# Bringing the 32-by-32 blocks of a turned node pair with eight 128-partition transfers instead of four 32-partition ones, in a graph layer on one Trainium2 core

## What is computed

```python
msg  = x[src]
agg  = segment_sum(msg, dst, num_segments=n)
deg  = segment_sum(ones, dst, num_segments=n)
mean = agg / maximum(deg, 1)[:, None]
h    = mean @ W_l + b + x @ W_r
x    = layernorm(x + h * sigmoid(h))
```

## Time and profile before

| | |
|---|---|
| time, median of 3 runs | 1550.5 us (1549.07 to 1550.78) |
| the profiled execution's own time | 1550.07 us |
| its span, first to last instruction | 1548.2 us |
| granted TensorE clock, mean of the span | 0.989 of full speed |
| PE busy in the span | 1501.8 us (97%) |
| DVE, ACT, POOL busy | 1319.6, 1184.4, 1030.7 us |
| bytes moved by DMA | 397.68 MB, mean 257 GB/s |

### The profile page before, as it was taken

The page is one execution under the profiler, slowest core; times in us unless marked ns, Lnnn a source line. Parts: engine busy times, 40 slices in busy tenths (PEclk is TensorE's granted clock), DMA queues, the critical chain, the costliest instruction groups (busy, mean ns, idle before and its releaser), DMA issues.

```text
span 1548.2 us, 23957 instructions
## 1 busy us (share of the span) xinstructions
PE 1501.8 (97%) x7198; PEld 1244.3 (80%) x7198; DVE 1319.6 (85%) x2088; ACT 1184.4 (77%) x1609; POOL 1030.7 (67%) x1097
## 2 busy tenths in 40 slices
PE   7799999999999899999999999999999999999996
PEld 6687778888887787888888888888888888888884
DVE  7699999999998777888888888888888888888886
ACT  4354433333334698999999999999999999999996
POOL 6466556656662766667767777677677776776673
PEclk9899999999999999999999999999999999999998
DMA  5656589989997689999999999999999999999995
GB/s 193 173 178 192 166 247 266 266 259 272 267 267 232 176 258 265 277 283 276 276 271 268 280 298 270 281 287 273 268 281 281 289 280 279 280 277 275 290 270 184
DMA packets 298965, 397.68 MB, mean 257 GB/s; under 512 B 42652, under 2 KB 144822, under 8 KB 298837
## 3 DMA queue, kind: packets, MB, share of 16 engines
q1 hardware_dynamic: 250855, 321.43, 69.6%
q0 software_dynamic: 46944, 74.22, 18.0%
q10 hardware_dynamic: 1038, 0.50, 0.1%
HBM read 335.97 MB, written 139.67 MB: 307 GB/s over the span
## 4 chain that ended last, share of the span: by engine, by line
PE 80%; ACT 5%; DMA 5%; issue 4%; DVE 4%; POOL 1%; SPq 1%; POOLq 0%; ACTq 0%; DVEq 0%
PE pH L529 72%; PE pT L633 4%; PE pT L602 3%; DMA cor<-correction_rows,node_idx 2%; ACT O L804 2%; ACT cor L750 1%; PE pT L540 1%; ACT pH L816 1%; DMA X<-in_x 1%; POOL cor L441 1%; DMA light_x<-in_x 1%; DVE Z L904 1%; ACT Z L828 0%; DMA xs<-in_x 0%; DMA wr_raw<-in_L_gnn_W_r 0%
## 5 line engine op out<-in xcount | busy, mean ns | idle before, releaser
L441 POOL DMA_INDIRECT cor<-correction_rows,node_idx x347 | 395.7, 1140 | 224.8 <-ACT cor L750 150.1
L529 PE MATMUL pH<-ws_hi,x_hi 128*128 128x512 f32 x876 | 348.3, 398 | 7.6 <-ACT pH L816 4.5
L529 PE MATMUL pH<-ws_hi,x_lo 128*128 128x512 f32 x876 | 343.9, 393 | 0.0
L529 PE MATMUL pH<-ws_lo,x_hi 128*128 128x512 f32 x876 | 343.4, 392 | 0.0
L529 PE MATMUL pH<-wb_hi,x_hi 128*128 128x512 f32 x688 | 276.1, 401 | 0.0
L529 PE MATMUL pH<-wb_hi,x_lo 128*128 128x512 f32 x688 | 268.9, 391 | 0.0
L529 PE MATMUL pH<-wb_lo,x_hi 128*128 128x512 f32 x688 | 268.5, 390 | 0.0
L804 ACT ACTIVATE O<-Z,shift,rstd 128x512 f32<-128x512 f32 x347 | 261.9, 804 | 3.6 <-DVE shift L1127 3.6
L1117 DVE BATCH_NORM_STATS2 stats<-Z 128x6 f32<-128x512 f32 x347 | 219.3, 673 | 0.3 <-issue 0.3
L1109 DVE TENSOR_TENSOR Z<-Z,X 128x1024 f32<-128x1024 f32 x174 | 211.2, 1214 | 2.8 <-ACT Z L828 2.8
L725 ACT ACTIVATE s_hi<-sums 128x512 fp32r<-128x512 f32 x98 | 62.0, 633 | 192.3 <-DVE sums L1028 192.3
(11 more groups left out here) (148 smaller groups left out, 2765.1 us busy)
## 6 DMA issues: line engine op xcount, KB each, us to landing
X<-in_x SPq DMA_DIRECT2D x173, 512.0 KB, 4.6
out<-O SPq DMA_DIRECT2D x173, 512.0 KB, 5.3
xs<-in_x SPq DMA_DIRECT2D x344, 128.0 KB
correction_rows<-c_out SPq DMA_DIRECT2D x98, 256.0 KB, 4.2
light_x<-in_x SPq DMA_DIRECT2D x58, 256.0 KB, 2.8
light_h<-early_product SPq DMA_DIRECT2D x44, 256.0 KB
out<-light_o SPq DMA_DIRECT2D x44, 256.0 KB, 4.3
join_row<-joined SPq DMA_DIRECT2D x98, 64.0 KB, 4.1
```

What stands on the lines that cost most here:

```text
L441: g.indirect_dma_start(out=out_, out_offset=None, in_=table, in_offset=bass.IndirectOffsetOnAxis(ap=idx, axis=0), bounds_check=bound, oob_ ...
L529: last = mm(ps, a[:, k], w[:, k], start=(n == 0 and not onto), stop=(n == len(terms) - 1), skip_group_check=onto)
```

## The change

`load_blocks` brings the same 1024 runs with eight transfers instead of four. Before, transfer j (of four) filled the 32 partitions 32j to 32j + 31, eight runs in each. Now transfer i (of eight) writes run i of all 128 partitions: from the 32 rows 32i to 32i + 31 of the pair it takes, for j = 0 to 3 and r = 0 to 31, row r's columns 128j to 128j + 127, and lays them on partition 32j + r. The bytes that arrive, and where, are the same. Each transfer still counts 16 on `blocks_in`, so `turn_blocks` waits for 128 a pair instead of 64.

```diff
             def load_blocks(t):
                 wait(sp, blocks_turned, (t + 1) // 2 - 1)
                 first = BASE + 2 * t * P
-                for j in range(4):
-                    sp.dma_start(x_raw[32 * j:32 * j + 32].rearrange("r a (i c) -> r (a i) c", i=4),
-                                 x[first:first + 2 * P, j * P:(j + 1) * P].rearrange("(i r) c -> r i c", r=32)
+                for i in range(8):
+                    sp.dma_start(x_raw[:, i // 4, i % 4 * P:(i % 4 + 1) * P],
+                                 x[first + 32 * i:first + 32 * i + 32].rearrange("r (j c) -> j r c", j=K)
                                  ).then_inc(blocks_in, 16)
...
             def turn_blocks(t, q, u):
-                dve.wait_ge(blocks_in, 64 * ((t + 1) // 2))
+                dve.wait_ge(blocks_in, 128 * ((t + 1) // 2))
```

## The result

The changed kernel takes 1713.7 us (1712.49 to 1715.96) against 1550.64 us for the kernel before beside it: a ratio of 1.1054, 95% interval 1.1037 to 1.107. It is slower by 163 us. The forecast was 1893 us, with a range of 1740 to 2170, so the direction was right and the size was out by more than half: the loss is 163 us and not 343. Whether the reason given was right is what the experiments test.

A forecast was written before the change was run, and what follows sets the result against it. PE and DMA engines were both taken as full at 11.76 us a period; four engines carrying all blocks would need 15.75 us, so 86 x 3.99 = 343 us on 1550 gave 1893 us, range 1740 to 2170.

The forecast's parts named there:

- The bound before: Kernel before, 700 to 1500 us: PE busy 799.83 of 800 us, DMA engines 97%; a period of 11.76 us.
- how a transfer is shared out: Block transfers, source count 4 against destination 128: four engines carry all 1024 packets, twelve none; chance 0.82.
- the 256 block packets on a full engine: Each of four engines carries 256 packets of 512 bytes a period, priced between 28.3 and 62 ns each.
- the 7.42 us: An engine's work in a period without blocks: 6.42 us of 2 KB packets and 1.00 us of other queues.
- The lower end: Period on the four engines if all block packets run at the quick windows' 28.3 ns: 7.42 + 7.24 = 14.66 us.
- The upper of the two ends: Period if nothing else on these engines gets quicker: 11.40 us plus 192 more packets at 28.3 ns, 16.83 us.
- restarts after each turn: Block transfers on the four engines: restarts speak against the low end, so the middle, 15.75 us, was taken; no separate size.
- The issues: SP's eight block issues a turned pair in place of four: 4.0 us, hidden under the transfers, counted as 0.
- Where the stall went: `turn_blocks` on DVE waits for blocks some 300 us, in nearly all 86 turns; behind it `x_lo`, then PE.
- Sixteen engines without loss: Rival: block transfers cut in 16, DMA share falls to 79%, PE stays full, 1543 to 1550 us; chance 0.06.
- Sixteen engines and late issues: Rival: block transfers cut in 16, the last of eight issued 2.0 us later, 43 us lost, 1593 us; chance 0.06.
- Four engines at the slow price: Rival: all block packets on four engines at 62 ns, 23.3 us a period, 2540 us; chance 0.06.

The follow-up runs named there:

- All sixteen-engine variants: Source's outermost count 16, or 128 at both ends, in the changed kernel; kernel before cut in eight transfers, reordered 0, 2, 1, 3, or reordered with second buffer: ratios 0.9982 to 1.0024.
- the one with eight engines: Changed kernel with the source's outermost loop counting 8 in place of 4, runs dealt to other partitions: 1556.18 us, ratio 1.0056.
- Counts of 16, 8, 4 and 2: Source's outermost loop count; 4 is the changed kernel, the others deal its runs to the partitions in another order: ratios 1.0004, 1.0056, 1.1054, 1.4584.
- with two engines: Changed kernel with the source's outermost loop counting 2 in place of 4, runs dealt to other partitions: 2257.2 us, ratio 1.4584.
- six-of-eight kernel: Changed kernel with six of its eight transfers kept and two given an outermost source count of 16: 1622.29 us, ratio 1.0478.
- with two buffers: Changed kernel with a second buffer for x_raw and a semaphore for each, so next blocks are fetched before DVE empties the first: 1711.36 us, ratio 1.1057.
- the old shape: Kernel before with its pattern of 32 partitions a transfer cut in eight transfers, outermost count 32 at both ends: 1552.97 us, ratio 1.0024.

## Why the prediction was right and wrong

**The bound before** was read rightly: PE full, DMA engines at 97%. All sixteen-engine variants stand within 0.3% of before, the one with eight engines within 0.6%.

**The deciding term, how a transfer is shared out,** was right. Counts of 16, 8, 4 and 2 give 1549.89, 1556.18, 1713.7 and 2257.2 us. The rule that the Trainium skill states in "DMA: Bandwidth & Descriptors", section "Why a DMA increments its semaphore by 16 and not by 1" (the largest number of engines, up to 16, that divides both outermost counts) agrees with all four; which engines they are, no row shows.

**The step that failed is the size of one term of the sum: the 256 block packets on a full engine.** By choosing 15.75 us the prediction gave them 15.75 - 7.42 = 8.33 us, 32.5 ns each. The period of 13.75 us leaves them 6.33 us, 24.7 ns each, if the 7.42 us are kept. The 2.0 us between make 86 x 2.0 = 172 of the 179 us by which the forecast was too high. They came in two parts.

- The price, 0.9 us. The lower end took 28.3 ns, the length of a packet's record, as the time that an engine is taken up. In the 2 us of blocks alone 333 packets ran on four engines: one started every 2000 / (333 / 4) = 24.0 ns on each, while the records are at most 0.289 x 32 us / 333 = 27.8 ns long. In the longer stretches one starts every 4700 / (717 / 4) = 26.2 ns, and with two engines every 5000 / (372 / 2) = 26.9 ns, with records of some 29 and 30 ns. In all three the packets start closer together than a record is long, so neighbouring records overlap. The slope from four to two engines says 24.8 ns. With that the six-of-eight kernel, which was not used for it, comes to 7.42 + 208 x 0.0248 = 12.58 us, against 12.68 measured. By the 26 to 27 ns of the longer stretches a part of the 0.9 us would be in the 7.42 us and not in the price; no run separates the two. The rows had shown the overlap: the one queue q1 fills 116.2% of the engines' time in the earlier trace rows. The expectations above still took a common 1.06 for it.
- The choice between the ends, 1.09 us. The lower end, 14.66 us, would have given 1799 us; the middle added the other 94. The upper of the two ends kept the old, slow price for 64 of the 256 packets, and "restarts after each turn" were held against the lower one. Neither shows: the changed kernel's packets run at less than the quick price, and with two buffers, where SP hardly waits for the turn, the time is the same (1711.36 us).

Even the range's lower bound, 13.9 us a period, lay 0.15 us above the truth. With 24.8 ns the prediction's own sum is 13.77 us and its time 1550 + 86 x (13.77 - 11.76) = 1723 us. Counted from the 11.91 us that the whole stage had, in place of 11.76, it would be 1710 us.

**The issues** were counted at 4.0 us a pair and 0 in the sum. They take 8 x 0.757 = 6.1 us, and the 0 was right: with sixteen engines eight issues cost nothing (1.0004 and 0.9994) or some 4 us (the old shape).

**Where the stall went** was half right. DVE's wait was forecast at some 300 us in nearly all turns and is 170.5 in 45; beside it stands PE's wait of 117.4 us for `X`, which was not priced. With two engines that wait is 507.5 us, so it grows with the load of the few engines. The rate was forecast at 209 GB/s and is 241, which follows from the shorter period (280 x 11.76 / 13.75 = 239). PE's share was forecast at 75% and is 90%, the DMA share at 59% and is 73%; at 13.75 us the same formulas give 86% and 67%, so the period explains only the larger part of these two. The rest of the DMA share is in the records of the 2 KB packets: q1's 66.1% of 12800 us, less 466 x 128 block packets of 27.8 ns, leaves some 95 ns for each of its 71,300 packets of 2 KB, where the prediction took 84.5.

**The rivals.** Sixteen engines without loss happened where sixteen engines were given: 1549.89 us and no gain in time, as that rival said, but with a DMA share of 88% and not 79%. Sixteen engines and late issues: 0 to 4 us instead of 43. Four engines at the slow price: the packets ran at less than the quick one.

## What to carry to other kernels

Before a transfer is rearranged, read the outermost loop of both its ends: a count of 4 at one end, as here at the source, put it on four DMA engines, and the other transfers then waited for these four, while the mean DMA share fell from 97% to 73% and looked like relief. Where a share can exceed 100%, records overlap, so price a packet by how many start in a window that holds nothing else, not by the length of one. And a chain of waits without a gap may be only the place where a full resource shows: cut it once before you blame it.

## What the runs showed of the hardware

- The number of DMA engines follows the outermost count of the end with the smaller one: with 2, 4 and 8 against 128, blocks alone filled 2.2, 4.4 and 7.6 engines' worth; with 16 and 8 PE stays the bound, 4 and 2 gave periods of 13.75 and 20.10 us.
- A full engine starts a 512-byte read of HBM every 24.0 to 26.9 ns (three stretches; the slope over two kernels is 24.8 ns), while the packet's record is 28 to 30 ns long.
- SP's issue takes 433 ns with 128 at both ends and one run a partition, 497 ns with 32 at both ends and eight runs, 599 ns with 16 against 128, and rises to 757 ns with four and 1667 ns with two engines.
- The same bytes, brought on sixteen engines by eight transfers over 128 partitions in place of four over 32, take the DMA share from 97% to 88%, with no gain in time where PE is the bound.
